# Moving the last two elementwise steps of a head's output from VectorE to GpSimd

## The reference

```python
qkv = jnp.einsum('bte,fe->btf', x, Wqkv).reshape(B, T, H, 3 * D)
q, k, v = jnp.split(qkv, 3, axis=-1)          # then heads first; q = q + pe, k = k + pe
scores = jnp.einsum('bhtd,bhsd->bhts', q, k) / jnp.sqrt(D)
scores = jnp.where(causal, scores, -jnp.inf)
probs = jax.nn.softmax(scores, axis=-1)
attn = jnp.einsum('bhts,bhsd->bhtd', probs, v)
out = jnp.einsum('btf,ef->bte', attn.transpose(0, 2, 1, 3).reshape(B, T, H * D), Wo)
```

## Time and profile before

| | |
|---|---|
| median of three runs | 825.11 us |
| span of the profiled execution | 830.6 us |
| mean granted TensorE clock | 0.932 |
| TensorE busy | 701.2 us, 84% |
| VectorE busy | 653.0 us, 79% |
| ScalarE busy | 534.4 us, 64% |
| GpSimd busy | 477.2 us, 57% |
| attention stage, 48 to 630 us | 582 us |

### The profile page before, as it was taken

One profiled execution on the slowest core, in us unless ns is written; L12 is line 12 of the kernel. 1 busy time (PEld: TensorE's weight loads), 2 busy tenths in 40 slices (PEclk: granted clock), 3 DMA queues, 4 the chain that ended last, 5 costly groups with the idle time before them and its releaser, 6 DMA issues. The chain is left out here.

```text
span 830.6 us, 11252 instructions
## 1 busy us (share of the span) xinstructions
PE 701.2 (84%) x3247; PEld 519.9 (63%) x3247; DVE 653.0 (79%) x1111; ACT 534.4 (64%) x786; POOL 477.2 (57%) x259
## 2 busy tenths in 40 slices
PE   5888898799889778987987898799996879988883
PEld 4555666576667556765765666576775768766651
DVE  3779778987977887798868789977856888895774
ACT  4757676676857566775767577666672657675661
POOL 6045675467547545764755476567693345666660
PEclk9989999899989989998989899999998999999995
DMA  6000000000000000000000000000050000000000
GB/s 164 1 1 1 1 0 2 1 1 1 1 1 1 0 0 0 1 0 1 0 1 0 0 0 0 0 0 1 1 165 1 1 1 1 1 0 13 13 0 25
DMA packets 11326, 8.44 MB, mean 10 GB/s; under 512 B 2930, under 2 KB 10003, under 8 KB 11155
## 3 DMA queue, kind: packets, MB, share of 16 engines
q1 hardware_dynamic: 11282, 7.96, 3.5%
HBM read 6.84 MB, written 1.05 MB: 9 GB/s over the span
## 5 line engine op out<-in xcount | busy, mean ns | idle before, releaser
L298 POOL TENSOR_TENSOR probs_l<-probs,probs_h 128x1024 fp32r<-128x1024 f32 (+1 forms) x160 | 360.7, 2258 | 251.8 <-PE o_ps L603 162.2
L417 DVE TENSOR_REDUCE m_part<-max_ps 128x1 f32<-128x512 f32 (+2 forms) x320 | 179.2, 600 | 90.6 <-PE max_ps L544 80.5
L349 ACT ACTIVATE probs<-scores 128x1024 f32<-128x1024 f32 (+1 forms) x160 | 150.8, 942 | 151.4 <-PE scores L579 89.3
L603 PE MATMUL o_ps<-probs_h,v 128*128 128x512 f32 (+5 forms) x640 | 201.8, 401 | 4.9 <-ACT o_sum L342 4.1
L544 PE MATMUL max_ps<-k,q 128*128 128x512 f32 (+2 forms) x320 | 114.0, 423 | 67.9 <-DVE m_part L417 35.8
L352 ACT ACTIVATE probs_h<-scores 128x1024 fp32r<-128x1024 f32 (+1 forms) x160 | 149.9, 937 | 0.0
L578 PE MATMUL scores<-q,k 128*128 128x512 f32 (+1 forms) x320 | 128.3, 401 | 0.0
L603 PE MATMUL o_ps<-probs_l,v 128*128 128x512 f32 (+1 forms) x320 | 124.5, 389 | 0.0
L603 PEld LDWEIGHTS o_ps<-probs_h,v 128*128 128x128 f32 (+1 forms) x640 | 103.1, 175 | 31.7 <-issue 6.3
L579 PE MATMUL scores<-q,k 128*128 128x512 f32 (+1 forms) x320 | 121.2, 379 | 0.0
L544 PEld LDWEIGHTS max_ps<-k,q 128*128 128x128 f32 x320 | 60.9, 201 | 95.5 <-DVE m_part L417 51.7
(11 more groups left out here) (203 smaller groups left out, 1114.3 us busy)
## 6 DMA issues: line engine op xcount, KB each, us to landing
v_all<-L_ffn_ew SPq DMA_DIRECT2D x2, 768.0 KB, 7.9
pos<-positions SPq DMA_DIRECT2D x1, 1024.0 KB, 6.7
out<-v_all SPq DMA_DIRECT2D x4, 256.0 KB, 2.3
acc<-L_attn_Wqkv SPq DMA_DIRECT2D x2, 256.0 KB, 3.9
v_all<-L_attn_Wo SPq DMA_DIRECT2D x2, 256.0 KB, 6.5
q<-m_row SPq DMA_DIRECT2D x32, 2.0 KB
v_all<-L_ffn_aw SPq DMA_DIRECT2D x2, 256.0 KB, 3.0
acc<-L_attn_Wqkv SPq DMA_DIRECT2D x2, 128.0 KB, 3.9
```

The source lines that it names most:

```text
L298: pool.tensor_tensor(probs_l[:, p % 2, :, lo:CH], probs[:, p % 2, :, lo:CH], probs_h[:, p % 4, :, lo:CH], ALU.subtract).then_inc(S["probs_ ...
L349: act.activation(probs[:, p % 2, :, lo:CH], scores[:, p % 2, :, lo:CH], ACT.Exp, scale=D ** -0.5).then_inc(S["probs_ready"], 1)
L417: dve.tensor_reduce(m_part[:, r, j:j + 1], max_ps[:, u % 2, 0:width], AX.X, ALU.max).then_inc(S["tile_max_ready"], 1)
L603: last = pe.matmul(o_ps[0:rows, lo:CH], v, pr, start=(p == PAIR0[c] and j == 0 and k == 0), stop=(p == PAIR0[c + 1] - 1 and j == 1 and k = ...
```

## The change

GpSimd issues the multiplication and the subtraction of each chunk, in the same slots s + 1 and s + 3 as VectorE did, ahead of that slot's probs_l. Its section gets an argument `prev`, and one more section behind the last head for chunk 3 of that head. The tiles, shapes and signals are the same. On GpSimd the subtraction is followed by a wait for its own signal, and preceded by one for the signal of its latest probs_l.

```diff
@@ GpSimd
-            def section(g, cur, nxt):
+            def section(g, cur, nxt, prev):
                 for p in range(NP):
+                    for c, ahead in due(DONE, p, 1, cur, nxt, prev):
+                        h = plus(g, ahead)
+                        pool.wait_ge(S["inverse_turned"], at(h, NC, c + 1))
+                        wait(pool, S["head_out_low_ready"], at(h, NC, c - 1))
+                        pool.tensor_tensor(o_norm[:, c % 2, :], o_sum[0:D, :], l_rows, ALU.mult).then_inc(S["head_out_normalised"], 1)
+                    for c, ahead in due(DONE, p, 3, cur, nxt, prev):
+                        h = plus(g, ahead)
+                        pool.wait_ge(S["head_out_high_ready"], at(h, NC, c + 1))
+                        pool.wait_ge(S["probs_low_ready"], at(g, NP, p if cur else 0))
+                        pool.tensor_tensor(oh[D:P, c % 2, :], o_norm[:, c % 2, :], oh[0:D, c % 2, :], ALU.subtract).then_inc(S["head_out_low_ready"], 1)
+                        pool.wait_ge(S["head_out_low_ready"], at(h, NC, c + 1))
                     if cur:
...
-            section((0, -1), False, True)
-            section((0, 0), True, True)
+            section((0, -1), False, True, False)
+            section((0, 0), True, True, False)
             with pool.Fori(0,(H - 2) // 2) as i:
                 for o in (1, 2):
-                    section((i, o), True, True)
-            section((0, H - 1), True, False)
+                    section((i, o), True, True, True)
+            section((0, H - 1), True, False, True)
+            section((0, H), False, False, True)
@@ VectorE
-                    for c, ahead in due(DONE, p, 1, cur, nxt, prev):
-                        h = plus(g, ahead)
-                        dve.wait_ge(S["inverse_turned"], at(h, NC, c + 1))
-                        wait(dve, S["head_out_low_ready"], at(h, NC, c - 1))
-                        dve.tensor_tensor(o_norm[:, c % 2, :], o_sum[0:D, :], l_rows, ALU.mult).then_inc(S["head_out_normalised"], 1)
                     if p in V_LOW and nxt:
                         v_low(plus(g, 1), V_LOW.index(p))
-                    for c, ahead in due(DONE, p, 3, cur, nxt, prev):
-                        h = plus(g, ahead)
-                        dve.wait_ge(S["head_out_high_ready"], at(h, NC, c + 1))
-                        dve.tensor_tensor(oh[D:P, c % 2, :], o_norm[:, c % 2, :], oh[0:D, c % 2, :], ALU.subtract).then_inc(S["head_out_low_ready"], 1)
```

## The result

The changed kernel takes 834.1 us (median of 20 runs, 827.9 to 839.0) beside 827.9 us for the kernel before (20 runs, 820.8 to 832.2): ratio 1.0068, 95% interval [1.0046, 1.0089]. It was forecast at 774 us; it is 0.7% slower. So the two profiles are read stall by stall here, and not by their spans.

What follows compares the result with a forecast made beforehand. No engine is full; TensorE's waits for VectorE, blocked behind GpSimd, were taken as the bound. Stalls and clock -50.8, slots 4 and 6 -1.4, end +1.2 sum to -51.0 us: 774 us from the median, range 757 to 812.

Steps and rivals of the forecast that it cites:

- Its new waits: GpSimd's queue: waits ahead of probs_l cost nothing, covered by idle time; 0.3 to 1 us per head if not.
- Slot 11: TensorE's 2.55 us stall, ended by the low part of q: 2.25 us goes per head, bounds 0 and 2.55.
- Slot 9: TensorE's 2.91 us stall for a maximum: 2.0 us goes per head, 0.9 stays, bounds 0 to 2.91.
- Clock: Two 3.4 us half-speed stretches per head behind the stalls: 3.0 us regained per head, bounds 0 and 3.4.
- Short waits in dense work leave the clock up: Clock term's ground: the 1.25 us wait at slot 6 is followed by no half-clock stretch.
- The price on GpSimd: Each of the 64 moved 64x512 instructions takes 1.28 us on GpSimd, bounds 0.73 and 2.35.
- the rival of the GpSimd price: Rival 3, slower: a moved GpSimd instruction costs 2.5 us or more, which eats the gain; chance 0.09.
- Slots 4 and 6: TensorE's waits for ScalarE's output copy and for the subtraction: net -0.2 us a head, 1.4 us gained; bounds +1.5 and -0.6.
- The end: Serial work behind the last pair: two GpSimd steps of 1.28 us for 0.68 add 1.2 us.
- 83%, no bound by sum: Attention stage: 82 us added brings GpSimd to 443 us in about 531, so its total work is no bound.
- rival 2: No change: something equally late ends the stalls, ScalarE's exponentials or k copies; 817 to 833 us, chance 0.08.
- Rival 1: Shared port, half given back: low part of q in slot 10 meets probs_l, slot 11 stall stays; 801 us, chance 0.14.

Runs made afterwards that it cites:

- the kernel with the pause: The changed kernel plus a GpSimd wait for the multiplication's own signal before it goes on to probs_l: 788.8 us, ratio 0.952 to the kernel before.

## Why the prediction was wrong

**The step that failed** is *Its new waits*: "I cost these waits at nothing, because GpSimd's idle time covers them". In the seven heads with maxima the idle time did cover what GpSimd had to do. It had another use that the prediction did not price: in slot 9 it was the opening through which VectorE read its two-input operands. Before's low part of k in head 3, VectorE:

```profile
309.79 0.67 DVE L456 TENSOR_TENSOR k<-qk,k 64x512 fp32r<-64x512 f32 x1
```

It comes where GpSimd's 4.93 us of idle time end: 0.08 us behind the start of the probs_l at 309.71 in head 3, and 0.06 to 0.64 us ahead of that start in the other six. It took 0.67 us in all seven, and in head 3 it was the probs_l that lost time (3.00 us for 2.35). In the changed kernel the multiplication stands there already, and is joined on to two probs_l. The price was 5.3 us on VectorE (5.95 - 0.67), and all of it arrived at TensorE.

**Slot 11** inherited that. Forecast: 2.25 of 2.55 us goes. Measured: the stall rose to 5.34 to 5.60, so 3.0 us worse instead of 2.25 better. The step looked at the low part of q alone (L461) and counted at most one probs_l per blocked instruction, because the blocked rows that it read ended some 0.55 us behind the one probs_l that they stood behind. With the pause or with 128 partitions the stall is 0.97 us in head 3, for 0.3 forecast; of the 0.7 between them 0.6 may answer to the low part of k, which still waits for the multiplication (1.29 for 0.67; an estimate, no run takes it apart).

**Slot 9** held in size, and partly by luck. 0.9 us was to stay, because the low part of q ahead of the maxima would keep its 2.70 us. It did not: in slot 7 it takes 0.68 to 1.31 us in the changed kernel, and slot 9 has no wait in any of the seven heads. What stays is a wait of 0.29 to 0.90 us in slot 10, whose maxima stand behind the sums' copy of slot 8 (2.24 us in head 3, behind a probs_l). In the kernel with the subtraction alone 0.90 stays.

**Clock**: 3.0 of 3.4 us a head was to come back; nothing did. Two stretches of 3.4 us became one of 6.8. In the kernel with the pause the time at half clock is 51.2 us less than before (75.1 to 23.9), 15 stretches of 3.4 us where 14 were forecast. At half speed that is 25.6 us of lost work, 3.7 a head, against 3.0 forecast and a bound of 3.4. The bound left out the stretches behind slot 6: before has one in heads 1, 3 and 5, behind waits of 1.01 us there, so "Short waits in dense work leave the clock up" was read from one head and does not hold in all.

**The price on GpSimd** held: 1.27 and 1.39 us for 1.28, with another operation and with other partitions, so the rival of the GpSimd price is out. The subtraction's rows are 1.26 to 1.29, or 1.53 to 1.55 where it first waits for VectorE.

**Slots 4 and 6** held: -1.4 us forecast. TensorE's wait for ScalarE's copy fell from 4.1 to 1.0 us in the stage, its wait for the subtraction rose from 6.7 to 8.5: -1.3.

**The end** was half the cost. The serial tail is 6.40 for 5.18 us, the +1.2 as laid out. But the whole last head lost 5.2 us, since with no maxima GpSimd sets the pace there, and the moved instructions have no cover. The sum "83%, no bound by sum" was an average over heads of two kinds.

**The rivals.** The time came out 1 us above rival 2 (no change, 817 to 833, chance 0.08), but not by its mechanism. ScalarE ended neither stall. Rival 1 named the right resource, in the wrong place: the low part of q in slot 10 took 0.69 us, and what blocked was the low part of k a slot earlier, for three instructions and not for one.

The Trainium skill speaks against the change in Perfetto Trace Analysis, Optimizing Scalar/DVE Operations ("might not help"), and the prediction set that beside rows and went by the rows. The changed kernel agrees with the page (1.007), the same change with its multiplication over 128 partitions does not (0.949). The prediction's account of what the moved work is worth was about right in size: 51 us forecast, 42 measured with the wide multiplication (828.2 to 785.8), and 3.7 to 5.5 more when the last head's steps go back to VectorE (782.4 to 778.7, 834.1 to 828.6).

## What to carry to other kernels

When work is moved to GpSimd, list every two-input VectorE instruction that now falls within it, also those that never waited before; idle time of GpSimd is their opening, so count it as used. A copy can be held up too: the sums' copy took 0.42 us in slot 8 of before's head 3 and 2.24 us, behind a probs_l, in the changed kernel. Do not put a GpSimd instruction over 64 partitions directly ahead of others: widen it to 128 if the extra rows are harmless (it costs the same here), or wait for its signal (0.22 us). Read utilisation for each kind of stage: the last iteration, which lacks the prefetch of the next, may be bound by another engine.

## What the hardware showed that was not expected

**A read that stays closed across instructions.** A VectorE instruction with two SBUF inputs, behind a 64-partition multiplication on GpSimd that was followed without a gap by 128-partition probs_l, took 3.65 us with one of them and 5.95 with two; with 0.22 us of pause behind the multiplication 1.29, and behind a 128-partition multiplication 1.28. The same without the narrow instruction is in before: two probs_l back to back, and VectorE gets in at the boundary. GpSimd and VectorE of the kernel before, early in the attention:

```profile
48.16 4.03 POOL L298 TENSOR_TENSOR probs_l<-probs,probs_h 128x1024 fp32r<-128x1024 f32 x2 [34.25 <-ACT probs_h L352]
```
```profile
48.19 2.86 DVE L461 TENSOR_TENSOR q<-qk,q 64x512 fp32r<-64x512 f32 x1
```

VectorE's ends at 51.05, over a microsecond before the pair does.

The Trainium skill, SBUF — State Buffer, section SBUF: two separate sides, has the pair held for one instruction. The boundary at 48.16 to 52.19 agrees with that; the 5.95 us across three instructions do not, and there the measurement decides.

**Why**, is inferred and not shown. The Trainium skill, GPSIMD Engine Reference, section Instruction dispatch, says that a core of GpSimd serves 16 fixed partitions and goes on to the next instruction when its own share is done. If the half of the cores that a 64-partition instruction leaves idle is ahead of the other half from then on, some core is always reading, and the port has no moment in which it is free; a pause brings them together. The runs with and without the pause, the width and the second step fit this, but no row shows a single core. Whether an instruction on the upper 64 partitions, or one as wide but shorter, does the same was not tried.

**Width cost nothing on GpSimd.** Multiplying 512 columns takes 1.26 to 1.30 us over 64 and over 128 partitions, and subtracting them into the other 64 partitions takes 1.26 to 1.29. Other lengths were not compared over both widths.
